# Attention taken by pairs of heads: float32r scores in the two halves of TensorE's rows, maxima 1024 wide, exponentials 512 wide, maxima moved by DMA

## What is computed

```python
DIM, HEADS = 256, 16            # HEAD_DIM = 16, x is (1, 4096, 256)
q = _split_heads(x @ Wq.T + bq)
k = _split_heads(x @ Wk.T + bk)
v = _split_heads(x @ Wv.T + bv)
scores = jnp.einsum('hbnd,hbmd->hbnm', k, q) * SCALE    # 1/sqrt(256)
attn = jax.nn.softmax(scores, axis=-1)
out = jnp.einsum('hbnm,hbmd->hbnd', attn, v)
```

## Time and profile before

| | |
|---|---|
| median of 3 runs | 5356.41 us (5352.18 to 5356.89) |
| span of the profiled execution, first to last instruction | 5345.3 us |
| the profiled execution with what lies around its span | about 5356 us: the median stands 11.1 us above the span, and no other figure is given for that one execution |
| mean granted TensorE clock | 0.966 |
| TensorE busy | 4971.2 us (93%) |
| VectorE, ScalarE, GpSimd busy | 3786.1, 3177.2, 998.8 us |
| steps of the attention | 229.7 to 3233.0 us |
| projection ahead of it | 20 to 189 us |

### The profile page before, as it was taken

How to read it: one execution, slowest core, us unless ns; L and a number is a source line. 1 busy time by engine, 2 the same in 40 slices (tenths; PEclk the granted TensorE clock), 3 DMA queues, 4 the chain that set the end, 5 groups by cost and what they waited for, 6 DMA issues and landing times. The chain is left out here.

```text
span 5345.3 us, 87655 instructions
## 1 busy us (share of the span) xinstructions
PE 4971.2 (93%) x25432; PEld 2447.3 (46%) x25432; DVE 3786.1 (71%) x5840; ACT 3177.2 (59%) x3780; POOL 998.8 (19%) x1827
## 2 busy tenths in 40 slices
PE   6799999999999999999999995999986379999999
PEld 4333233233232332332332333777755257777777
DVE  5888888888888888888888885655544544444444
ACT  3477677677677776776776774444454344444444
POOL 0032332332232332332233230000000000000000
PEclk8899999999999999999999997999998689999999
DMA  3201110110111011011011102000010410000000
GB/s 121 73 21 27 25 27 21 25 27 21 25 27 25 21 27 27 19 27 27 19 26 27 26 19 84 24 24 31 12 33 17 106 37 12 12 12 12 12 12 12
DMA packets 159086, 157.94 MB, mean 30 GB/s; under 512 B 69216, under 2 KB 125200, under 8 KB 157200
## 3 DMA queue, kind: packets, MB, share of 16 engines
q1 hardware_dynamic: 138352, 121.31, 8.7%
q0 software_dynamic: 20480, 33.60, 2.6%
HBM read 91.83 MB, written 37.75 MB: 24 GB/s over the span
## 5 line engine op out<-in xcount | busy, mean ns | idle before, releaser
L758 DVE TENSOR_REDUCE PM<-A 128x1 f32<-128x512 f32 x4140 | 2572.5, 684 | 434.3 <-PE A L643 424.8
L727 ACT ACTIVATE PR<-SB 128x1024 f32<-128x1024 f32 x2050 | 1987.2, 1021 | 840.0 <-PE SB L652 827.4
L643 PE MATMUL A<-QST,KA 96*128 96x512 bf16 x4140 | 1588.3, 384 | 18.3 <-DMA QST<-QS 17.4
L652 PE MATMUL SB<-KB,QST 99*128 99x512 bf16 x4100 | 1571.3, 383 | 24.7 <-issue 23.8
L664 PE MATMUL PV<-PR,VH 128*32 128x512 f32 x8192 | 1117.2, 607 | 0.0
L652 PEld LDWEIGHTS SB<-KB,QST 99*128 99x128 bf16 x4100 | 400.6, 98 | 1259.0 <-ACT PR L727 848.4
L643 PEld LDWEIGHTS A<-QST,KA 96*128 96x128 bf16 x4140 | 404.2, 98 | 490.4 <-DVE PM L758 222.3
L1912 DVE TENSOR_TENSOR m_h_lo<-m_h_full,m_h_hi 128x512 fp32r<-128x512 f32 x320 | 221.6, 693 | 285.2 <-ACT m_h_hi L1817 284.9
L810 POOL DMA_DIRECT2D OG<-OS x384 | 194.8, 511 | 1086.5 <-ACT OS L745 1084.7
L1817 ACT CAST m_h_hi<-m_h_full 128x512 fp32r<-128x512 f32 x320 | 198.5, 620 | 245.5 <-DVE m_h_full L1909 243.4
L1909 DVE TENSOR_TENSOR m_h_full<-m_h_full,m_c 128x512 f32<-128x512 f32 x256 | 175.3, 685 | 235.3 <-ACT m_h_full L1811 204.8
(11 more groups left out here) (291 smaller groups left out, 6014.5 us busy)
## 6 DMA issues: line engine op xcount, KB each, us to landing
OG<-OS POOLq DMA_DIRECT2D x384, 64.0 KB, 1.9
QST<-QS SPq DMA_DIRECT2D x102, 128.0 KB, 4.3
KA<-KS SPq DMA_DIRECT2D x780, 16.0 KB, 1.6
KB<-KS SPq DMA_DIRECT2D x774, 16.0 KB, 1.6
m_x<-X3T SPq DMA_DIRECT2D x16, 512.0 KB, 3.7
QS<-parts SPq DMA_DIRECT2D x16, 384.0 KB, 2.6
KS<-parts SPq DMA_DIRECT2D x16, 384.0 KB, 2.6
x_tok<-in_L_attn_x SPq DMA_DIRECT2D x8, 512.0 KB, 4.4
```

The source lines that it names most:

```text
L643: nc.tensor.matmul(A[:, a_slot(u) % A_BANKS, :], KA[0:STACK, par, i * P:(i + 1) * P], QST[0:STACK, slot, j * TB:(j + 1) * TB], start=True, ...
L652: mm = nc.tensor.matmul(SB[:, pair % 2, e, :], QST[0:ROWS, slot, m * P:(m + 1) * P], KB[0:ROWS, par, :], start=True, stop=True)
L727: nc.scalar.activation(PR[:, pair % 4, :, :], SB[:, pair % 2, :, :], ACT.Exp, scale=SCALE).then_inc(b_free, 1)
L758: nc.vector.tensor_reduce(PM[:, par, i, j:j + 1], A[:, a_slot(u) % A_BANKS, :], AX.X, ALU.max).then_inc(a_free, 1)
```

## The change

Everything is by pairs of heads now: 8 pairs x 8 blocks = 64 steps, each with the work of two steps of before.

- Queries and keys are kept in two float32r parts (`PARTS = 2`). `mid` and the second VectorE operation of each chunk go.
- A head's stack is three products of 16 rows, 48 rows, plus two rows of maxima. Head 0 of the pair lies in partitions 0 to 49, head 1 in 64 to 113 (`HALF`). Each matmul of scores uses the 64 rows of one half.
- One ring `KST` of four key blocks serves both passes, in place of `KA` and `KB`.
- Pass A: `units_a` issues the two heads' units into two neighbouring banks of four, and VectorE takes both maxima with one instruction over 2 x 512.
- Pass B: chunks into three banks in turn, one exponential of 512 for each.
- The maxima are split into two parts on GpSimd and go by four small DMAs on SyncE's queue straight into the rows of the keys. For that, unit i of pass A takes every fourth key, so its weights are read with a stride of four elements.
- Two of the four quarters of columns belong to each head. Two are added on GpSimd with one instruction, after two DMAs in place of three.
- The loop is 4 turns of 16 steps, each step written out.

The core of the diff:

```diff
-PARTS = 3
+PARTS = 2
...
-                def mid(i, slot, c):
-                    act.wait_ge(rest_ready, count(i * 4 + (c + 1)))
-                    nc.scalar.copy(parts[slot][:, c, 1, :], rest[:, c % 2, :]).then_inc(mid_ready, 1)
...
-K_PARTS = (0, 0, 0, 1, 1, 2)
-Q_PARTS = (0, 1, 2, 0, 1, 0)
+K_PARTS = (0, 0, 1)
+Q_PARTS = (0, 1, 0)
+STACK = len(K_PARTS) * HD
+HALF = P // 2
+LEAD = 8
+EXPS = 2 * MC
+PVS = MC // 2
+S_BANKS = 3
+K_SLOTS = 4
+P_SLOTS = 8
+
+def s_bank(v):
+    return (v if v < 4 else v + 2) % S_BANKS
+
+def s_before(v):
+    for w in range(v - 1, v - EXPS, -1):
+        if s_bank(w % EXPS) == s_bank(v):
+            return w
...
+                def load_shift(b, nb):
+                    sp.wait_ge(neg_low, count(b + 1))
+                    for e in range(2):
+                        for j in range(PARTS):
+                            row = e * HALF + STACK + j
+                            sp.dma_start(KST[row:row + 1, nb % K_SLOTS, :].bitcast(F32),
+                                         NM[:, nb % 2, j, e * TT:(e + 1) * TT].bitcast(F32),
+                                         allow_slow_non_contiguous=True).then_inc(shift_loaded[nb % 2], 16)
+
+                def step(t, pair, hp, nb, following):
+                    sp.wait_ge(s_done, count(t * EXPS))
+                    alone(sp, passed)
+                    if nb + 3 < NB:
+                        load_k(pair, nb + 3)
+                    else:
+                        load_k(following, nb + 3 - NB)
+                    if nb == 0:
+                        load_q(following, 1 - hp)
+                    load_shift(t + 1, (nb + 1) % NB)
...
+                def unit_a(u, e, nb, slot):
                     i, j = divmod(u, NB)
+                    rows = slice(e * HALF, e * HALF + STACK)
+                    keys = KST[rows, nb % K_SLOTS, :].rearrange("r (p i) -> r i p", i=TT)[:, i, :]
+                    return nc.tensor.matmul(A[:, u % 2 * 2 + e, :], keys, QST[rows, slot, j * TB:(j + 1) * TB],
+                                            start=True, stop=True)
+
+                def units_a(b, u, nb, slot):
+                    pe.wait_ge(a_free, count(b * MC + (u + 1)))
+                    unit_a(u, 1, nb, slot)
+                    unit_a(u, 0, nb, slot).then_inc(a_done, 1)
+
+                def unit_s(t, c, e, nb, slot):
+                    v = 2 * c + e
+                    rows = slice(e * HALF, e * HALF + ROWS)
+                    pe.wait_ge(s_free, count(t * EXPS + (s_before(v) + 1 + S_BANKS)))
+                    nc.tensor.matmul(SB[:, s_bank(v), :], QST[rows, slot, c * P:(c + 1) * P],
+                                     KST[rows, nb % K_SLOTS, :], start=True, stop=True).then_inc(s_done, 1)
+
+                def values(t, k, slot):
+                    if k == 0:
+                        pe.wait_ge(pv_read, count(t))
+                    pe.wait_ge(s_free, count(t * EXPS + (4 * k + 4 + S_BANKS)))
                     for r in range(4):
+                        c, e = 2 * k + r // 2, r % 2
+                        at = HALF * e + 2 * HD * (c % 2)
+                        mm = nc.tensor.matmul(PV[at:at + 2 * HD, :], VH[:, slot, e, c, :],
+                                              PR[:, (2 * c + e) % P_SLOTS, :], start=(k == 0), stop=(k == PVS - 1))
                     mm.then_inc(p_free, 1)
...
+                def step(two, hp, nb):
+                    t = number(two, hp, nb)
+                    for q in range(2, MC + 2):
+                        ahead, u = divmod(q + LEAD, MC)
+                        ...
+                        if q == MC:
+                            block = hp * NB + nb + 1
+                            pe.wait_ge(shift_loaded[s_nb % 2], count((two * 8 + (block // 2 + 1)) * SHIFT))
+                        unit_s(s_t, q % MC, 0, s_nb, s_slot)
+                        units_a(t + ahead, u, a_nb, 1 - hp if past else hp)
+                        unit_s(s_t, q % MC, 1, s_nb, s_slot)
+                        if q % 2 == 1:
+                            ...
+                            values(t, q // 2 - 1, hp)
...
+                def exp(t, v):
+                    if v % 4 == 0:
+                        act.wait_ge(p_free, count(t * PVS + (v // 4 + 1)))
+                    act.wait_ge(s_done, count(t * EXPS + (v + 1)))
+                    nc.scalar.activation(PR[:, v % P_SLOTS, :], SB[:, s_bank(v), :], ACT.Exp,
+                                         scale=SCALE).then_inc(s_free, 1)
...
+                def unit_max(b, u, par):
                     i, j = divmod(u, NB)
+                    dve.wait_ge(a_done, count(b * MC + (u + 1)))
+                    nc.vector.tensor_reduce(PM[:, par, :, i, j:j + 1], A[:, u % 2 * 2:u % 2 * 2 + 2, :], AX.X,
                                             ALU.max).then_inc(a_free, 1)
```

More of the change, by code:

```diff
@@ L584, in in_steps @@
+        shift_loaded = [sem(f"shift_loaded{i}") for i in range(2)]
+        groups_moved, o_stored = sem("groups_moved", from_zero=True), sem("o_stored", from_zero=True)
+        LOAD = 16 * 2 * len(K_PARTS)
+        SHIFT = 16 * 2 * PARTS
+        P_AHEAD = P_SLOTS // 4
         def in_steps(eng, body):
-            with eng.Fori(0, HEADS // 2) as pair:
+            with eng.Fori(0, HPAIRS // 2) as two:
                 for hp in range(2):
[L590 to L594, removed]
+                    for nb in range(NB):
+                        body(two, hp, nb)
@@ L599, in _ @@
             def _(sp):
[L600 to L607, removed]
@@ new lines, in _ @@
+                load_q(0, 0)
+                load_k(0, 1)
+                load_k(0, 2)
+                load_shift(0, 0)
+                sp.wait_ge(rows_set, count(2))
+                with sp.Fori(0, HPAIRS // 2 - 1) as two:
+                    for hp in range(2):
+                        for nb in range(NB):
+                            step(number(two, hp, nb), two * 2 + hp, hp, nb, two * 2 + (hp + 1))
+                for hp in range(2):
+                    pair = HPAIRS - 2 + hp
+                    for nb in range(NB):
+                        step(pair * NB + nb, pair, hp, nb, (pair + 1) % HPAIRS)
@@ L631, in _ @@
             @block.tensor
             def _(pe):
-                def unit_a(block, u, par, slot):
+                def unit_a(u, e, nb, slot):
                     i, j = divmod(u, NB)
[L636 to L644, removed]
-                                     start=True, stop=True).then_inc(a_done, 1)
@@ new lines, in step @@
+                def step(two, hp, nb):
+                    t = number(two, hp, nb)
+                    for v in range(4, EXPS):
+                        exp(t, v)
+                    for v in range(4):
+                        exp(t + 1, v)
+                    act.wait_ge(p_free, count((t + 1) * PVS + P_AHEAD))
+                    act.wait_ge(os_free, count(t + 1))
+                    nc.scalar.copy(OS[:, nb % 2, :], PV[:, :]).then_inc(pv_read, 1)
+                act.sem_inc(s_free, S_BANKS)
@@ L751, in _ @@
+                for v in range(4):
+                    exp(0, v)
                 in_steps(act, step)
@@ L773, in _ @@
                 block_max(STEPS, 0)
-                for u in range(12):
+                for u in range(LEAD + 2):
                     unit_max(STEPS + 1, u, 1)
```

350 lines of the change are left out of this document (119 added, 231 removed).

## The result

The changed kernel takes 5073.77 us (median of 4 runs, 5072.1 to 5077.41) beside 5356.65 for the kernel before; the ratio is 0.9476, 95% interval 0.9462 to 0.9489. It is faster by 283 us. The forecast was 4940, so the gain was 419 as forecast and is two thirds of that as measured. The measured time lies in the stated range of 4780 to 5300 and above the likeliest case's own, 4820 to 5065, by 9. It falls where the prediction had put rivals 2 and 4 (5065 to 5320, 0.17), though neither of them happened as written.

The account below looks back on a forecast made before the run. The prediction took the loop of waits between ScalarE and TensorE as the bound, 2.475 us a group, 39.8 a step. Steps -420, turns -21, start +27, projection -5 gave -419 from 5356.4: 4940 us, range 4780 to 5300.

Parts of the forecast that it names:

- likeliest case: Whole kernel: the loop between ScalarE and TensorE sets the pace; 4820 to 5065 us, chance 0.62.
- rivals 2 and 4: TensorE's weights cost more than 0.11 us (5065 to 5320), or the maxima's DMA lands late (5130); together 0.17.
- chunk until its result shows 0.39: Pass B link in the loop: from a chunk's matmul on TensorE until its result shows, 0.39 of 2.475 us.
- the bound of 2.6: Upper bound of the loop: one more load not done ahead per mode change, slower strided loads; 41.8 us a step.
- Turns: Outer loop of the attention: three turns in place of seven, 5.3 us each, 21 us less.
- The start: Before the first exponential: first maxima 17 us more, `QST` and its load 7, shift by DMA 3; together 27 more.
- The projection: Four casts and four VectorE subtractions less per 512 tokens; 5 us less for all eight blocks, from 0 to 20.
- The maxima by DMA: Maxima sent to the key rows: 7.7 to 9.2 us within 11.1, hidden by 2 to 3 us.
- Rival 1: TensorE's scores: the two halves don't overlap, group 2.95 us, step 47.4, about 5425 us, slower; chance 0.11.
- Rival 2: TensorE: strided reads or loads not ahead, a pair 0.35 to 0.44, group 2.6 to 2.85, 5065 to 5320; shared chance 0.17.
- Rivals 3 and 4: VectorE bounds, 36.7 a step, 4740 (0.07 including times up to forecast); or maxima land in 7 us, 5130 (shared 0.17).
- Rival 5: TensorE's clock falls to the lower level in the attention: group 3.7 us, about 6150 us; chance 0.03.

Follow-up runs that it names:

- x1: Changed kernel with the two parts of queries, keys and maxima in bfloat16 in place of float32r: 4852.42 us.
- x5: Changed kernel with each matmul of scores over both halves of the rows, so none runs beside another, maxima sent as zeros: 5536.86 us.

## Why the prediction was right, and where it was too good

- **The bound after the change** was named rightly: the loop between ScalarE and TensorE over three banks. The group shows its links one by one, the reordering costs 129 us, and more work on VectorE costs only 14.
- **The step that was mis-sized** is the loop's term "chunk until its result shows 0.39". Its source was a bfloat16 chunk at 1501.77 in the earlier trace rows. The chunk that now follows the products carries a float32r load of its own and shows 0.50 (x1 puts it back to 0.39). I had charged that load once, 0.09 for the gated chunk, and named a second one only in the bound of 2.6 (41.8 a step), which is where the kernel landed. The row that showed it was in the same group that I took the 0.09 from: 0.48 at 4703.59 beside 0.40 at 4703.91. The other links: hand over 0.04 for 0.06, gated chunk to products 0.42 for 0.40, products to chunk 0.99 for 1.00, exponential 0.605 for 0.595, ScalarE's start 0.04 for 0.03. The sum is 2.60 for 2.475, and the step 41.92 for 39.8, which is 64 x 2.12 = 136 us too few.
- **Turns:** three in place of seven was right, the price was not. I took 5.3 us from the old loop. A turn now costs 8.3, since two or three groups and not one run on the lower clock, and 13 of the 21 us forecast came (38 less 25).
- **The start:** from the first issue of the attention to the first exponential it was 37.6 us and is 66.6, 29 more for 27 forecast. The maxima of the first block take 36.30 us as worked out.
- **The projection** gives 5.3 us (the attention's first DMA issue at 183.87 in place of 189.17) for 5.
- **Sum by spans:** -285 for the steps, -13 for the turns, +29, -5 is -274 against the measured -269.8. The last 4 are not assigned. Against the forecast of -419 the spans are 149 us short: 136 by the step, 8 by the turns, 2 by the start and the rest unassigned. By the medians the time is 134 above the forecast, because the median of the kernel before stood some 9 us over its profiled execution, and that of the changed kernel 4 under its own.
- **The maxima by DMA** are hidden: they land in 2.0 us, not in the 3.4 that I leaned to, and TensorE's waits list none for them.
- **Rival 1** has its side confirmed by x5, its price not (5537 for 5425; most of the extra is the load behind the products, which I left out there too). It did not happen: the halves start 0.01 us apart. Its sum was also off by a little, as 8 x 0.23 + 1.09 is 2.93 and not 2.95.
- **Rival 2** did not happen as written: a pair of matmuls stays at 0.24 us (1502.73 to 1502.97), and the stride does cost 0.12 us a load, but outside the loop. What came is its milder cousin in the bounds, a second load in the loop that is not done ahead. Its lower end was argued badly, as a pair at 0.35 gives a group of 2.49, which is below the 2.6 written there.
- **Rivals 3 and 4** did not happen: VectorE idles 0.25 us a group, and TensorE waits for none of the maxima.
- **Rival 5** did not happen here, with 0.99 over the steps. A clock at the lower level for the whole attention came in two of the experiments, and more easily than the 0.03 that I gave it suggests. The changed kernel's group there is 4.07, where the prediction had 3.7.

The rule of the Trainium skill (TensorE: Matmul & The Clock Gate, Weight-path perf modes) that fast weight load is off for FP32 was dismissed in the prediction as changing no term. The trace agrees that the float32r loads are the longer ones (0.188 us for 0.098). With bfloat16 loads the time falls by 221 us (5074 to 4852), of which some 203 lie in the steps, by the two loads per group that no other work covers. Whether that rule is what makes them longer no run separates.

The Trainium skill (TensorEngine Tiling (Array Packing), Key Properties) says that tiles operate independently and in parallel; the trace agrees (0.01 us between the starts of the two halves), and the run over all rows puts some 450 us on it.

## What to carry to other kernels

When no engine is full after a change, write the loop of waits through the buffers link by link, and for each link take a row of the same type and in the same position. A weight load that waits for a bank, or that stands behind the products, is not the load that runs ahead: here each cost 0.10 to 0.11 us. Then look for cheap ways to shorten a link: bfloat16 parts for float32r ones gave 221 us here, at a price in precision, while plain in place of strided loads, which lie off the loop, gave nothing. And a cut of TensorE's work can cost more than it saves where the granted clock then stays low (5208 us for a forecast of 4756), so look at the granted clock of each stretch first.

## What the runs showed of the hardware that I had not expected

- TensorE's clock stayed at 0.50, 1.2 GHz, for the whole attention in two versions that count 99 to 100% of the time as busy: all scores on one half of the rows (8108 us), and products with bfloat16 exponentials and values in place of float32 ones (5208 us). In each, the stretch ahead of the steps ran at the lower level, as it does in every version here, and the steps never lifted it. Serial matmuls over 112 and 114 rows run at 1.00. What exactly lifts it these runs don't settle. The stretch ahead of the steps in the changed kernel, and in the version with short products:

```profile
200.00:240.00 40.00, 25.87 (x66) 10.05 (x66) 35.50 (x32) 0.00 (x0) 0.00 (x0) 0.50 0.07 11
200.00:240.00 40.00, 26.20 (x66) 10.16 (x66) 35.82 (x32) 0.00 (x0) 0.00 (x0) 0.50 0.07 10
```

- A float32r load of 128 columns shows 0.188 us, and 0.306 with a stride of four elements.
- After a stop for instructions (ScalarE idle 4.0 to 4.2 us) the float32r version runs two or three groups of 4.07 us before it is back at 2.60. The bfloat16 version stops for less (2.4 to 2.8 us) and has one group of 3.4 to 3.7 us in place of 2.39, then at most 0.5 us more in the next.
